# A softmax edge pass on one Trainium2 core: five of seven classes of the 0/1 rows made on ScalarE, and five and four columns in turn looked up on TensorE

## The reference, cut to what matters

```python
z = x @ Wn
s_src = (z @ att_src)[src]; s_dst = (z @ att_dst)[dst]; s_edge = (edge_attr @ We) @ att_edge
score = leaky_relu(s_src + s_dst + s_edge, negative_slope=0.2)
score_exp = exp(score - max_per[dst])
alpha = score_exp / (segment_sum(score_exp, dst) + 1e-08)
out = segment_sum((z[src] + edge_attr @ We) * alpha[:, None], dst)
```

## Time and profile before

| | |
|---|---|
| median of 3 runs | 13509.75 us (13502.95 to 13512.86) |
| span of the profiled execution | 13509.6 us |
| VectorE busy | 11066.4 us (82%) |
| TensorE matmuls busy | 9536.4 us (71%) |
| GpSimd busy | 9266.9 us (69%) |
| ScalarE busy | 4374.5 us (32%) |

### The profile page before, as it was taken

One profiled execution on the slowest core, in us unless ns is written; L12 is line 12 of the kernel. 1 busy time (PEld: TensorE's weight loads), 2 busy tenths in 40 slices (PEclk: granted clock), 3 DMA queues, 4 the chain that ended last, 5 costly groups with the idle time before them and its releaser, 6 DMA issues. The chain is left out here.

```text
span 13509.6 us, 209667 instructions
## 1 busy us (share of the span) xinstructions
PE 9536.4 (71%) x57073; PEld 8046.3 (60%) x57073; DVE 11066.4 (82%) x24500; ACT 4374.5 (32%) x14847; POOL 9266.9 (69%) x9348
## 2 busy tenths in 40 slices
PE   5666667777757766777774546886886888678886
PEld 4555556666645555555552116886886777567775
DVE  8888878888768888888888997886886888589997
ACT  3444434444423333333333331111111111123332
POOL 6777757777667777777774005777776777677776
PEclk8888879999878888888886667998997999699997
DMA  3333324444323333333335761221221222133332
GB/s 89 89 89 85 88 71 125 124 119 124 113 65 100 99 101 101 101 100 97 99 101 195 272 246 41 48 47 39 47 48 38 50 49 49 30 78 87 85 87 68
DMA packets 637171, 1243.59 MB, mean 92 GB/s; under 512 B 206033, under 2 KB 390390, under 8 KB 586530
## 3 DMA queue, kind: packets, MB, share of 16 engines
q1 hardware_dynamic: 322624, 912.21, 19.9%
q0 software_dynamic: 300160, 269.02, 11.8%
q10 hardware_dynamic: 14337, 61.82, 1.2%
HBM read 475.84 MB, written 768.08 MB: 92 GB/s over the span
## 5 line engine op out<-in xcount | busy, mean ns | idle before, releaser
L1030 PE MATMUL p_slots<-part,one_lo 128*128 128x208 f32 (+1 forms) x18032 | 2666.9, 312 | 616.3 <-DVE one_lo L1048 615.9
L990 POOL DMA_INDIRECT rows<-gcn_table,index x2450 | 2442.6, 997 | 883.0 <-issue 727.7
L1030 PEld LDWEIGHTS p_slots<-part,one_lo 128*128 128x128 f32 x18032 | 2584.2, 205 | 699.2 <-DVE one_lo L1048 682.7
L1351 PE MATMUL a_p_slots<-att_part,a_one_lo 128*128 128x456 f32 x8232 | 2007.5, 408 | 585.2 <-DVE y L1414 502.8
L1351 PEld LDWEIGHTS a_p_slots<-att_part,a_one_lo 128*128 128x128 f32 x8232 | 1741.4, 214 | 953.6 <-DVE y L1414 680.7
L1282 POOL DMA_INDIRECT sent<-a_out_rows,a_place x1568 | 1585.5, 1011 | 494.0 <-issue 476.2
L622 PE MATMUL p_slots<-x_part,key_lo 128*128 128x448 f32 x6916 | 1649.2, 393 | 109.7 <-DVE scratch L751 73.3
L556 POOL DMA_INDIRECT msg<-x_rows,index x1372 | 1312.0, 956 | 507.4 <-issue 448.4
L556 POOL DMA_INDIRECT msg<-h_rows,index x1274 | 1234.4, 969 | 490.9 <-issue 383.8
L622 PEld LDWEIGHTS p_slots<-x_part,key_lo 128*128 128x128 f32 x6916 | 1378.1, 206 | 226.3 <-DVE scratch L751 90.3
L788 DVE SCALAR_TENSOR_TENSOR run<-run,keep,msg 128x129 f32<-128x129 f32 (+1 forms) x3136 | 1112.8, 355 | 388.7 <-ACT msg L591 284.2
(11 more groups left out here) (478 smaller groups left out, 17203.7 us busy)
## 6 DMA issues: line engine op xcount, KB each, us to landing
running_dst<-a_run SPq DMA_DIRECT2D x98, 1600.0 KB
running_src<-s_run SPq DMA_DIRECT2D x98, 1600.0 KB
running<-run SPq DMA_DIRECT2D x98, 1032.0 KB
running<-run SPq DMA_DIRECT2D x98, 1024.0 KB
running<-y SPq DMA_DIRECT2D x98, 656.0 KB
s_rows<-sent ACTq DMA_DIRECT2D x98, 584.0 KB, 7.0
begun_x<-zeros SPq DMA_DIRECT2D x98, 512.0 KB
a_xdst<-begun_x SPq DMA_DIRECT2D x98, 512.0 KB
```

Source lines behind the costliest of these rows:

```text
L990: pool.indirect_dma_start(out=rows[h][:, KS[h] + k, :], out_offset=None, in_=table, in_offset=offsets(index[h][:, k:k + 1])).then_inc(gath ...
L1030: ins = nc.tensor.matmul(to, one_lo[h][:, q, e:e + P], flat(part[:, q, :, :]), start=q == 0 and part_no == 0, stop=q == CLASSES - 1 and pa ...
L1351: ins = nc.tensor.matmul(to[:, k, 0:WIDE_COLUMNS], one_lo[h][:, q, e:e + P], part[:, q, :], start=q == 0 and part_no == 0, stop=q == WIDE_ ...
```

## The change

ScalarE now makes classes 2 to 6 of the 0/1 rows (`WIDE_LIT, EARLY = 5, 3`), VectorE only classes 0 and 1 (`OWN`). For each class ScalarE computes the square of (2 x key - 2 x lane), with the new per-partition operand `lane_bias`, and then relu(1 - that) over all five classes in one instruction, in place. It does so for block n+2 while block n is at work: three squares ahead of the copy of the run rows, two squares and the relu pass behind it and the stagings. The index copy moves from ahead of the exponentials to behind the spread factors. Even blocks look up five columns in groups of 2, 2 and 1, odd blocks four in groups of 2, 1 and 1 (`KS = (5, 4)`), so that 11 and 12 columns are gathered. TensorE does two groups ahead of the transposes and one behind them, and begins a block when ScalarE's pass for it (`lit`) and the pick that frees the PSUM bank are done. VectorE's slot mask moves behind the second pick. SyncE loads the next keys when `lit` says that these are used. Two semaphores, `squared` and `lit`, and `lane_bias` (one small VectorE instruction at the program's start) are added. The core of the diff:

```diff
-    KS = (4, 4)
+    KS = (5, 4)
     GATHERED = [B - K for K in KS]
-    FIRST = 2
-    GROUPS = [[slice(0, FIRST), slice(FIRST, K)] for K in KS]
-    MOST = [FIRST, max(KS) - FIRST]
-    FIRST_MADE, ONE_HOTS = 1, 1 + WIDE_CLASSES
-    SECOND_MADE = ONE_HOTS + 8
-    SCORED = SECOND_MADE + 8
+    GROUPS = [(slice(0, 2), slice(2, 4), slice(4, 5)), (slice(0, 2), slice(2, 3), slice(3, 4))]
+    G = 3
+    OWN = WIDE_CLASSES - WIDE_LIT
+    FIRST_MADE, ONE_HOTS = 1, 1 + OWN
+    SECOND_MADE = ONE_HOTS + 7
+    THIRD_MADE = SECOND_MADE + 3
+    SCORED = THIRD_MADE + 8
     MADE = SCORED + 1
     per = MADE + 4
...
                 sp.wait_ge(stepped, INIT + per * (n - 1) + ONE_HOTS)
+                sp.sem_inc(sig["rounds"].sem, 1)
+                sp.wait_ge(lit.sem, lit.base + n + 1)
                 load_keys(h, n + 2)
...
+            def square(h, classes):
+                for q in classes:
+                    ins = nc.scalar.activation(one_lo[h][:, q, :], keys[h][:], ACT.Square, bias=sig["lane_bias"][:, q:q + 1], scale=2.0)
+                return ins
+            def light(h, n):
+                act.wait_ge(squared.sem, squared.base + n + 1)
+                nc.scalar.activation(one_lo[h][:, OWN:WIDE_CLASSES, :], one_lo[h][:, OWN:WIDE_CLASSES, :], ACT.Relu, bias=sig["ones"][:, 0:1], scale=-1.0).then_inc(lit.sem, 1)
             act.sem_inc(copied, 2)
             for h in range(2):
                 stage_index(h, h * B)
                 stage(h, h * B)
+            for h in range(2):
+                act.wait_ge(spread_keys[h], 16)
+                square(h, range(OWN, WIDE_CLASSES)).then_inc(squared.sem, 1)
+                light(h, h)
             with act.Fori(0, IT) as i:
                 for h in range(2):
                     n = 2 * i + h
-                    act.wait_ge(gathered[h], 16 * GATHERED[h] * (i + 1))
-                    stage_index(h, (n + 2) * B)
                     act.wait_ge(stepped, INIT + per * n + SCORED)
                     nc.scalar.activation(p_factor, exps[h][:, 0:B], ACT.Exp)
@@ -1771,29 +1787,45 @@
                     act.wait_ge(activated, 2 * n + 1)
                     nc.scalar.activation(carried[:, :, 1:B], repeat(factor[h][:, B + 1:2 * B], S), ACT.Copy).then_inc(activated, 1)
+                    act.wait_ge(gathered[h], 16 * GATHERED[h] * (i + 1))
+                    stage_index(h, (n + 2) * B)
+                    act.wait_ge(looked, G * (n + 2))
+                    act.wait_ge(spread_keys[h], 16 * (i + 2))
+                    square(h, range(OWN, OWN + EARLY))
                     act.wait_ge(stepped, INIT + per * (n + 1))
                     act.wait_ge(stored[h], 16 * (i + 1))
                     nc.scalar.activation(run_rows[h][:, :, 0:S], run[h][:].rearrange("p c b -> p b c"), ACT.Copy)
                     nc.scalar.activation(run_rows[h][:, :, S], top[h][:, 1:1 + B], ACT.Copy).then_inc(copied, 1)
                     stage(h, (n + 2) * B)
+                    square(h, range(OWN + EARLY, WIDE_CLASSES)).then_inc(squared.sem, 1)
+                    light(h, n + 2)
...
             def multiply(h, g):
-                for k in range(KS[h] - FIRST if g else FIRST):
-                    e = (g * FIRST + k) * P
+                cut, to = GROUPS[h][g], p_slots[(h + g) % 2]
+                for k in range(cut.stop - cut.start):
+                    e = (cut.start + k) * P
                     for q in range(WIDE_CLASSES):
                         for part_no, part in enumerate(parts):
-                            ins = nc.tensor.matmul(p_slots[g][:, k, 0:WIDE_COLUMNS], one_lo[h][:, q, e:e + P], part[:, q, :],
+                            ins = nc.tensor.matmul(to[:, k, 0:WIDE_COLUMNS], one_lo[h][:, q, e:e + P], part[:, q, :],
                                                    start=q == 0 and part_no == 0, stop=q == WIDE_CLASSES - 1 and part_no == len(parts) - 1)
                 ins.then_inc(looked, 1)
+            pe.sem_inc(looked, G)
             with pe.Fori(0, IT) as i:
                 for h in range(2):
                     n = 2 * i + h
-                    pe.wait_ge(stepped, INIT + per * (n - 1) + ONE_HOTS)
+                    pe.wait_ge(lit.sem, lit.base + n + 1)
+                    pe.wait_ge(stepped, INIT + per * (n - 1) + SECOND_MADE)
                     multiply(h, 0)
+                    pe.wait_ge(stepped, INIT + per * (n - 1) + THIRD_MADE)
+                    multiply(h, 1)
                     pe.wait_ge(stepped, INIT + per * (n - 1) + MADE + 1)
                     pe.wait_ge(loaded[h], 16 * (B // PACK) * (i + 1))
@@ -1801,12 +1833,13 @@
                         ins = nc.tensor.transpose(flat(attr[h][:, g * PACK:(g + 1) * PACK, :]), attr_t[h][:, g, :], sig["ident"][:])
                     ins.then_inc(turned, 1)
-                    multiply(h, 1)
+                    pe.wait_ge(stepped, INIT + per * n + FIRST_MADE)
+                    multiply(h, 2)
...
             def one_hots(h, step):
-                for q in range(WIDE_CLASSES):
+                for q in range(OWN):
                     step(nc.vector.tensor_scalar(one_lo[h][:, q, :], keys[h][:], sig["lanes"][:, q:q + 1], None, ALU.is_equal))
...
-                        many = KS[h] - FIRST if g else FIRST
-                        slots = p_slots[g][:, 0:many, 0:Z * WIDE_CLASS].rearrange("p k (c s) -> p k c s", s=WIDE_CLASS)
+                        many = GROUPS[h][g].stop - GROUPS[h][g].start
+                        slots = p_slots[(h + g) % 2][:, 0:many, 0:Z * WIDE_CLASS].rearrange("p k (c s) -> p k c s", s=WIDE_CLASS)
                         mask = one_hi[h][:, GROUPS[h][g], :].unsqueeze(2).broadcast_to([P, many, Z, WIDE_CLASS])
-                        step(nc.vector.tensor_tensor(picked[g][:, 0:many, :, :], slots, mask, ALU.mult))
+                        dve.wait_ge(looked, G * (n + 1) + g + 1)
+                        step(nc.vector.tensor_tensor(picked[g % 2][:, 0:many, :, :], slots, mask, ALU.mult))
                     def gather(g):
-                        step(nc.vector.tensor_reduce(rows[h][:, GROUPS[h][g], 0:Z], picked[g][:, 0:KS[h] - FIRST if g else FIRST, :, :], AX.X, ALU.add))
+                        step(nc.vector.tensor_reduce(rows[h][:, GROUPS[h][g], 0:Z], picked[g % 2][:, 0:GROUPS[h][g].stop - GROUPS[h][g].start, :, :], AX.X, ALU.add))
...
-                    dve.wait_ge(staged[1 - h], i + 1 + h)
-                    one_slots(1 - h, step)
                     after(at=FIRST_MADE)
                     gather(0)
@@ -1867,11 +1898,16 @@
                     after()
                     step(nc.vector.tensor_tensor(edge_score[h][:], edge_score[h][:], at_dst[h][:], ALU.add))
-                    dve.wait_ge(looked, 2 * n + 2)
                     pick(1)
                     assert done[0] == SECOND_MADE
+                    dve.wait_ge(staged[1 - h], i + 1 + h)
+                    one_slots(1 - h, step)
+                    after(back=1)
+                    gather(1)
+                    pick(2)
+                    assert done[0] == THIRD_MADE
                     after()
-                    gather(1)
+                    gather(2)
...
```

More of the change, by code:

```diff
@@ L48 @@
 GROUP_SLOTS = 7
+WIDE_LIT, EARLY = 5, 3
 ON_CHIP = {16: (9, 8), 32: (6, 6)}
@@ L1672, in softmax_pass @@
         one_hi = [sb(f"e_one_hi{h}", [P, K, WIDE_CLASS]) for h, K in enumerate(KS)]
-        picked = [sb(f"e_picked{g}", [P, MOST[g], Z, WIDE_CLASS]) for g in range(2)]
+        picked = pair("e_picked", [P, 2, Z, WIDE_CLASS])
         rows = pair("e_rows", [P, B, C + 2])
@@ L1683, in softmax_pass @@
         run_rows = [scratch[:, h * B * W:(h + 1) * B * W].rearrange("p (b c) -> p b c", b=B) for h in range(2)]
-        p_slots = [ctx.enter_context(nc.psum_tensor(f"e_p_slots{g}", [P, MOST[g], 512], F32)) for g in range(2)]
+        p_slots = [ctx.enter_context(nc.psum_tensor(f"e_p_slots{g}", [P, 2, 512], F32)) for g in range(2)]
         p_attr = ctx.enter_context(nc.psum_tensor("e_p_attr", [P, 2 * B, EDIM], F32))
@@ L1691, in softmax_pass @@
         stepped, turned, activated, looked, copied = (sem(f"e_{n}") for n in ("stepped", "turned", "activated", "looked", "copied"))
+        squared, lit = sig["squared"], sig["lit"]
         block = ctx.enter_context(nc.Block())
@@ L1909, in _ @@
             nc.vector.tensor_copy(final[:, S:W], top[1][:, B:B + 1]).then_inc(stepped, 1)
+        squared.base += 2 * IT + 2
+        lit.base += 2 * IT + 2
 def complete_softmax(nc, sig, link, final, fix_at, running, ends, agg, groups, beside):
@@ L2035, in gnn @@
         sig = {n: Signal(ctx.enter_context(nc.semaphore(n))) for n in
-               ("copied", "turned", "turned_sb", "product", "saved", "fetched", "pe_step", "act_step", "dve_step", "pool_step", "moved", "rounds")}
+               ("copied", "turned", "turned_sb", "product", "saved", "fetched", "pe_step", "act_step", "dve_step", "pool_step", "moved", "rounds", "squared", "lit")}
```

(2 more changed lines are left out.)

1 line of the change is left out of this document (removed).

## The result

| | before | changed |
|---|---|---|
| median | 13506.35 us (13500.72 to 13512.86) | 13612.23 us (13606.80 to 13629.96) |
| span of the profiled execution | 13509.6 us | 13608.6 us |
| softmax pass, first to last scan | 1507.2 us | 1553.8 us |
| one block of it | 15.54 us | 16.02 us |

The account below looks back on a forecast made before the run. GpSimd's gathers were taken to bound the kernel before, ScalarE's round afterwards: 30.93 us plus 0.9 x 1.44 for the clock gives 16.11 a block, +56 us, and +4 ahead of the loop: 13,568 us, range 13,480 to 13,635.

Parts of the forecast that it names:

- case 1: Softmax pass: ScalarE's round with TensorE's clock falling sets the time; 13,568 us (13,545 to 13,590), chance 0.50.
- GpSimd as the bound before, VectorE right behind: Softmax pass before the change: GpSimd's 12 gathers set the 15.54 us block, with VectorE 0.4 us behind.
- ScalarE's round: Softmax pass: dependency chain through ScalarE, TensorE and VectorE around an even block, 30.93 us for two blocks, 15.47 a block.
- The clock: TensorE's even-block matmuls: behind a 3.3 us gap the granted clock drops nine times in ten, costing 1.44 us each.
- Ahead of the loop: Before the softmax loop: TensorE starts later, waiting for ScalarE's first five squares and pass; +4 us.
- The table load: ScalarE's load, now before the loop's exponential, runs ahead of its wait and costs nothing.
- case 5: ScalarE in the softmax pass: Square and Exp need separate tables, two loads a block; over 13,800 us, chance 0.03.
- The drain of 1.38 us: ScalarE's table load: by the Trainium skill a drain adds to the 1.28 us, so the rival would add 130 us.
- a table load on the path: Softmax pass: the load stands behind the exponential's wait, adding 63 us; 13,631 us, chance 0.10.
- Rival 3: Softmax pass: ScalarE's tail is shorter, the clock holds; 13,460 to 13,495 us, or 13,422 with GpSimd bound; chance 0.22.

Follow-up runs that it names:

- eleven: The kernel before with one gather less in every block (11 of 12), leaving one edge column in sixteen at zero; 13481.20 us, ratio 0.9980.
- bias_local: The changed kernel with lane_bias, its instruction and the semaphores made inside the softmax pass; 13561.94 us, ratio 1.0042.
- pad_only: bias_local plus an unused tile of 28 bytes where lane_bias stood; 13564.57 us, ratio 1.0043.
- squares_early: The changed kernel with the last two squares moved ahead of the copy of the run rows, relu pass left behind it; 13437.11 us, ratio 0.9946.
- step_only: bias_local plus one small VectorE instruction where the changed kernel makes lane_bias, no address moved; 13616.20 us, ratio 1.0083.
- pass_first: The changed kernel with all five squares and the relu pass moved ahead of the copy of the run rows; 13445.77 us, ratio 0.9953.

## Why the prediction was right, and where it was lucky

The forecast was 13,568 us, slower, in a range of 13,480 to 13,635; 13612.2 was measured. That is in the range, but above the 13,545 to 13,590 of the forecast's own case 1. The mechanism of case 1 was right and accounts for 52 of the 99 us; the other 47 it did not foresee, and that the sum with them still fell in the range was luck. Point by point:

- **GpSimd as the bound before, VectorE right behind**: right (eleven: 15.54 to 15.23 us with a gather less).
- **ScalarE's round**: right in each term to 0.15 us. Forecast and measured: arguments to copy 5.35 and 5.45; copy and stagings 2.81 and 2.78; two squares 1.54 and 1.58; relu pass 2.95 and 2.96; hand-over to TensorE 0.05 and 0.15; four columns at full clock 11.82 and 11.70 (12006.05 to the transposes at 12017.75); VectorE 5.87 and 5.88. TensorE's gap was put at 3.3 us and is 3.10. Between the starts of even blocks' matmuls the rounds with an undisturbed clock are 12036.96 - 12006.05 = 30.91 us, where 30.93 was forecast:

```profile
12006.05 11.86 PE L1814 MATMUL e_p_slots<-soft_part,e_one_lo 128*128 128x456 f32 x56 [3.08 <-DVE e_bounded L1919]
...
12017.75 0.38 PE L1833 MATMUL e_p_attr<-ident,e_attr_t 128*128 128x128 f32 x2
...
12036.96 11.87 PE L1814 MATMUL e_p_slots<-soft_part,e_one_lo 128*128 128x456 f32 x56 [3.09 <-DVE e_bounded L1919]
...
12067.88 13.43 PE L1814 MATMUL e_p_slots<-soft_part,e_one_lo 128*128 128x456 f32 x56 [3.10 <-DVE e_bounded L1919]
...
12100.36 13.29 PE L1814 MATMUL e_p_slots<-soft_part,e_one_lo 128*128 128x456 f32 x56 [3.10 <-DVE e_bounded L1919]
```

- **The clock**: right in kind. From 12067.88 to 12100.36 the round is 32.48 us, with 13.43 us for the 56 matmuls instead of 11.86, so this drop costs 1.57 where 1.44 was put; in the next round they take 13.29, and the two lengths come by turns. The drop comes behind 32 of the 40 gaps between 12000 and 13290 us, eight of ten and not nine. The other eight gaps are as long (3.08 to 3.10 us), so the length of the gap alone doesn't decide. Mean 32.04, 16.02 a block, forecast 16.11. The window view just behind the gap and in it:

```profile
12519.50:12522.50 3.00, 3.00 (x10) 0.57 0.17 29
...
12515.50:12518.50 3.00, 0.00 (x0) 1.00 0.86 266
```

In the trace of before, drops follow gaps of 1.8 us and more ahead of the transposes, behind about half of them. This one stands ahead of the 13.41 us in the earlier trace rows:

```profile
12516.93 0.54 PE L1801 MATMUL e_p_attr<-ident,e_attr_t 128*128 128x128 f32 x2 [1.80 <-DVE e_p_msg L1898]
```

Of its 15 gaps of 2.5 us and more, 12 and not 11 have a drop behind them, that at 12595.07 counted, and 3 and not 4 have none.

- **Ahead of the loop**: +4 forecast, +5.4 measured. 3.5 of these are TensorE's later start, which is what was forecast; the rest comes behind it, in the first block. Forecast for the pass alone: 13,568 (its own sum, 13509.7 + 60, is 13,569.7); bias_local and pad_only, which are the pass alone, gave 13,562 and 13,565.
- **The table load** costs nothing, as forecast; it runs 7 us before the exponential, ahead of the wait for the arguments:

```profile
12531.20 1.28 ACT L1785 ACT_TABLE_LOAD   x1
...
12538.17 0.19 ACT L1785 ACTIVATE e_p_msg<-e_exps 128x16 f32<-128x16 f32 x1 [5.69 <-DVE e_exps L1927]
```

There are 49 of them as before, so the squares bring no load of their own (case 5 is out). The Trainium skill ("ScalarE: Activation LUTs", Table-load gate) says "right before this ACTIVATE", and in the order of instructions that is so. In time the load here ran ahead of the activation's wait, and so it is hidden where the engine is early. The drain of 1.38 us, from which the forecast works out 130 us for a load behind the wait, doesn't show beside the loads of this pass: in the kernel before, the load of the earlier trace rows ends at 12529.77 + 1.28 = 12531.05, and the next activation starts at 12531.07:

```profile
12531.07 0.20 ACT L1750 COPY e_index<-src_i 128x12 int32 x1
```

- **Where it was wrong**: the sum took all outside the softmax pass as unchanged. It was 47 us longer, as much as the loop itself lost. No term stood for it, and the range held the time only because it had room for a table load on the path. The row of the granted clock in the page before reads 0.8 or less in the slices of the first spline pass and 0.9 in most of the second: these passes too don't have the full clock all the time, and that could have been a warning.
- **Rival 3** (a shorter tail makes the block 14.6) didn't come true, since the tail was as long as put, but was right as mechanism: with the tail taken off the path the block is 14.48 to 14.77 us.

## What to carry to other kernels

Idle time of an engine is no room for work unless it lies before the moment when the result is due: add up the round through all engines, with what stands ahead of the new work in each queue, not the engine's share. Work whose result another engine waits for goes ahead of work that only a store waits for. And where the granted clock of a stretch that nobody edited differs between programs, as here in the second spline pass, compare variants by the stretch that they touch as well as by the total.

## What the runs showed of the hardware that I had not expected

Behind TensorE's gap of 3.10 us the granted clock fell in 32 of 40 cases, and behind the gaps of 1.52 us and 0.8 us in squares_early in none, so that 1.5 us less waiting gave 2.6 us a round. Twelve matmuls whose result nobody reads were worth 0.59 us a block. And one VectorE instruction of 0.17 us near the start (at 30.6 us) went with 50 us in an unchanged pass 2 ms later, in the changed kernel and step_only nearly always, in the kernel before one time in ten, and in pass_first and squares_early mostly not.
